# Two common step lists of a two-layer transformer kernel are replaced by others

## The reference

```python
h = _layernorm(x) * (1 + ca) + sa                 # linear attention
qkv = h @ qkv_w + qkv_b                           # q, k, v in 16 heads of 16
q_prime, k_prime = elu(q) + 1.0, elu(k) + 1.0
context = einsum('bhld,bhlde->bhle', q_prime, cumsum(einsum('bhld,bhle->bhlde', k_prime, v)))
norm = einsum('bhld,bhld->bhl', q_prime, cumsum(k_prime))
x = x + ga * ((context / (norm + EPS)) @ out_w + out_b)

h = _layernorm(x) * (1 + cb) + sb                 # coupling network
gf = _global_net(h.mean(axis=1), ...)             # three small layers, one scalar
out = h
for _ in range(3):
    tf = _coupling_net(out, ...)                  # 256 -> 256 -> 128 -> 64 -> 1, gelu between
    coupling = 0.1 + adaptive_range * (0.7 * gf + 0.3 * tf - 0.5) * 2.0
    out = out + coupling * _twist(out)
x = x + gb * out
```

## Time and profile before

| | us |
|---|---|
| median of 3 runs | 1186.86 |
| lowest and highest | 1182.17, 1187.29 |
| profiled execution, its own time | 1183.12 |
| span of the profiled execution | 1181.3 |
| PE busy | 1068.3 (90%) |
| VectorE busy | 735.2 (62%) |
| ScalarE busy | 595.9 (50%) |
| POOL busy | 466.3 (39%) |

### The profile page before, as it was taken

One profiled execution on the slowest core, in us unless ns is written; L12 is line 12 of the kernel. 1 busy time (PEld: TensorE's weight loads), 2 busy tenths in 40 slices (PEclk: granted clock), 3 DMA queues, 4 the chain that ended last, 5 costly groups with the idle time before them and its releaser, 6 DMA issues. The chain is left out here.

```text
span 1181.3 us, 19797 instructions
## 1 busy us (share of the span) xinstructions
PE 1068.3 (90%) x6630; PEld 603.1 (51%) x6630; DVE 735.2 (62%) x1549; ACT 595.9 (50%) x1133; POOL 466.3 (39%) x692
## 2 busy tenths in 40 slices
PE   6699999999999998479999964899999998999996
PEld 3244554454454443346655532556666665455554
DVE  2867878787787783624333322767687873566756
ACT  3157667676767666013333323534444444877742
POOL 2444635444453511068788874433333410000000
PEclk9699999999999999589999996999999999999999
DMA  4521414233250411437676772021211002001001
GB/s 150 98 49 26 87 31 94 65 69 77 55 108 21 74 39 51 151 104 148 154 160 134 152 139 66 1 65 41 77 41 42 19 20 90 1 27 48 34 27 45
DMA packets 73540, 85.05 MB, mean 72 GB/s; under 512 B 12560, under 2 KB 67800, under 8 KB 73312
## 3 DMA queue, kind: packets, MB, share of 16 engines
q1 hardware_dynamic: 61088, 66.99, 21.9%
q0 software_dynamic: 12288, 16.79, 8.4%
q10 hardware_dynamic: 64, 0.02, 0.0%
HBM read 45.31 MB, written 25.21 MB: 60 GB/s over the span
## 5 line engine op out<-in xcount | busy, mean ns | idle before, releaser
L566 DVE TENSOR_REDUCE nmax<-psum 128x1 f32<-128x512 f32 (+3 forms) x352 | 215.5, 636 | 44.5 <-PE psum L790 39.6
L683 ACT ACTIVATE pT<-psum 128x512 f32<-128x512 f32 x320 | 181.1, 596 | 65.7 <-PE psum L811 35.6
L788 PE MATMUL psum<-k6T,q6T 96*128 96x512 bf16 (+3 forms) x512 | 128.3, 311 | 17.8 <-DVE nmax L566 13.5
L808 PE MATMUL psum<-q6T,k6T 99*128 99x512 bf16 x320 | 119.3, 382 | 1.1 <-ACT pT L683 0.9
L1093 POOL DMA_INDIRECT residual<-expert_y,idx_e x64 | 101.0, 1579 | 25.9 <-issue 18.0
L788 PEld LDWEIGHTS psum<-k6T,q6T 96*128 96x128 bf16 x512 | 45.9, 99 | 90.8 <-DVE nmax L566 57.8
L1612 DVE TENSOR_TENSOR l_scores<-psum,const_sb 128x512 f32<-128x512 f32 x128 | 79.5, 683 | 20.3 <-PE psum L1787 20.3
L790 PE MATMUL psum<-negs_bf,ident_bf 128*128 128x128 bf16 (+2 forms) x352 | 88.8, 252 | 0.0
L823 PE MATMUL psum<-pT,v 128*32 128x512 f32 x640 | 85.0, 604 | 0.0
L1080 POOL DMA_INDIRECT expert_tokens<-router_input,idx_e x64 | 63.0, 984 | 49.6 <-POOLq L913 30.4
L1745 PE MATMUL psum<-l_hT,l_w 128*128 128x512 f32 x128 | 63.7, 621 | 0.8 <-ACT l_plus_one L1689 0.8
(11 more groups left out here) (298 smaller groups left out, 2214.0 us busy)
## 6 DMA issues: line engine op xcount, KB each, us to landing
q6T<-q_parts SPq DMA_DIRECT2D x96, 128.0 KB, 4.4
expert_w<-in_ew SPq DMA_DIRECT2D x16, 768.0 KB
x_in<-in_x SPq DMA_DIRECT2D x8, 512.0 KB, 4.3
residual<-x SPq DMA_DIRECT2D x32, 128.0 KB, 1.9
router_input<-h SPq DMA_DIRECT2D x32, 128.0 KB, 1.8
l_x<-residual SPq DMA_DIRECT2D x8, 512.0 KB, 4.9
x_dram<-l_x SPq DMA_DIRECT2D x32, 128.0 KB, 1.7
out<-c_out SPq DMA_DIRECT2D x16, 256.0 KB, 2.1
```

What stands on the lines that cost most here:

```text
L566: dve.tensor_reduce(nmax[:, i, u * nh:(u + 1) * nh], ps_s[:, n % SR, 0:nh * (i + 1) * P].rearrange("p (h k) -> p h k", h=nh), AX_X, ALU.ma ...
L683: act.activation(pT[:, n % PR].rearrange("p h t -> p (h t)"), ps_t[:, n % TR, :], ACT.Exp, scale=HD ** -0.5).then_inc(probs, 1)
L788: pe.matmul(out[:, a, :], q6T[0:6 * HD, b % 2, u * nh + a, i * P:(i + 1) * P], k6T[0:6 * HD, b % 2, 0:w], start=a == 0, stop=False, skip_g ...
L808: last = pe.matmul(out, k6T[:, b % 2, j * P:(j + 1) * P], q6T[:, b % 2, hg * 4:hg * 4 + 4, i * P:(i + 1) * P], start=True, stop=j < i)
```

## The change

Both tables get other numbers. No instruction is added, removed or altered, and the functions that walk the lists stay the same. Since only the order of the sorted list counts, a shift of all numbers means nothing; what changes is the place of the steps relative to each other.

```diff
 LINEAR_PLACE = {
-    "ln": -322, "st": -318, "xn": -303, "hT": [-296, -289],
-    "qk": [-279, -273, -281, -277],
-    "v": [-283, -280, -275, -270],
-    "mask": [-276, -264], "nt": -262, "nb": [-255, -249],
-    "A": [-258, -252, -242, -233],
-    "kt": [-271, -265, -232],
-    "KV": [-251, -238, -225],
-    "PV": [-248, -236, -227, -221],
-    "pr": [-230, -223, -220, -218],
+    "ln": -16, "st": -11, "xn": 11, "hT": [14, 19],
+    "qk": [28, 32, 26, 30],
+    "v": [27, 31, 35, 45],
+    "mask": [36, 39], "nt": 42, "nb": [48, 53],
+    "A": [46, 51, 57, 65],
+    "kt": [34, 38, 43],
+    "KV": [44, 58, 73],
+    "PV": [54, 60, 69, 77],
+    "pr": [59, 76, 85, 88],
 }
 COUPLING_PLACE = {
-    "ln": -143, "st": -136, "xn": -132, "diag": -116,
-    "hT": [[-121, -118], [-112, -104]],
-    "g": {1: -98, 2: -89, 3: -76},
-    "PR": [[[-99, -100], [-114, -110]], [[-92, -96], [-69, -79]]],
-    "L2": [[-86, -83], [-61, -58], [-43, -42]],
-    "L3": [-75, -55, -39], "L4": [-71, -53], "tok": [-63, -45, -37],
-    "up": [[-67, -65], [-49, -46]], "r2": [-59, -60],
-    "fin": -34, "oT": [-33, -32, -30, -29, -26, -24, -9, -6],
+    "ln": -213, "st": -211, "xn": -201, "diag": -166,
+    "hT": [[-196, -189], [-187, -182]],
+    "g": {1: -177, 2: -170, 3: -156},
+    "PR": [[[-178, -181], [-184, -159]], [[-168, -175], [-150, -151]]],
+    "L2": [[-164, -162], [-142, -140], [-123, -121]],
+    "L3": [-158, -137, -119], "L4": [-155, -135], "tok": [-145, -126, -113],
+    "up": [[-149, -147], [-131, -128]], "r2": [-132, -144],
+    "fin": -112, "oT": [-109, -106, -104, -98, -95, -90, -77, -76],
 }
```

More of the change, by code:

```diff
@@ L1281 @@
 LINEAR_PLACE = {
[L1282 to L1285, removed]
-    "qk": [-279, -273, -281, -277],
-    "v": [-283, -280, -275, -270],
-    "mask": [-276, -264],
-    "nt": -262,
-    "nb": [-255, -249],
-    "A": [-258, -252, -242, -233],
-    "kt": [-271, -265, -232],
-    "KV": [-251, -238, -225],
-    "PV": [-248, -236, -227, -221],
-    "pr": [-230, -223, -220, -218],
+    "ln": -16,
+    "st": -11,
+    "xn": 11,
+    "hT": [14, 19],
+    "qk": [28, 32, 26, 30],
+    "v": [27, 31, 35, 45],
+    "mask": [36, 39],
+    "nt": 42,
+    "nb": [48, 53],
+    "A": [46, 51, 57, 65],
[3 more added lines that the diff above has]
+    "pr": [59, 76, 85, 88],
 }
@@ L1845 @@
 COUPLING_PLACE = {
[L1846 to L1849, removed]
-    "hT": [[-121, -118], [-112, -104]],
-    "g": {1: -98, 2: -89, 3: -76},
-    "PR": [[[-99, -100], [-114, -110]], [[-92, -96], [-69, -79]]],
-    "L2": [[-86, -83], [-61, -58], [-43, -42]],
[L1854 to L1860, removed]
+    "ln": -213,
+    "st": -211,
+    "xn": -201,
+    "diag": -166,
+    "hT": [[-196, -189], [-187, -182]],
+    "g": {1: -177, 2: -170, 3: -156},
+    "PR": [[[-178, -181], [-184, -159]], [[-168, -175], [-150, -151]]],
+    "L2": [[-164, -162], [-142, -140], [-123, -121]],
+    "L3": [-158, -137, -119],
+    "L4": [-155, -135],
+    "tok": [-145, -126, -113],
+    "up": [[-149, -147], [-131, -128]],
+    "r2": [-132, -144],
+    "fin": -112,
+    "oT": [-109, -106, -104, -98, -95, -90, -77, -76],
 }
```

## The result

| | before | after |
|---|---|---|
| median of 5 runs, us | 1186.28 | 1177.34 |
| lowest and highest | 1182.17, 1187.29 | 1176.96, 1180.3 |
| ratio, 95% interval | | 0.9947 [0.9929, 0.9965] |
| profiled execution, its own time | 1183.12 | 1177.1 |
| span | 1181.3 | 1175.3 |

The kernel became faster by 0.53%, some 6.3 us by the ratio and 6.0 by the two spans. A later repeat of the new kernel against the one before gave 0.9953 [0.9934, 0.9972]. The forecast was -1.9 us and 1185.0: the right side of zero, a third of the size. The median of 1177.34 lies 0.7 us under the low end of the range, 1178; the ratio, set against the 1186.28 of the kernel before, makes 1180.0, which is inside it. The gain of 0.53% lies at the 0.5% that was to part "within 0.5%" from "faster", and its interval (0.35% to 0.71%) doesn't say on which side.

A forecast was written before the change was run, and what follows sets the result against it. PE was taken as full in both stages' middles, so only gaps could change; -1.1 + 0.2 + 0.3 + 2.0 - 2.1 - 1.2 = -1.9 us gave 1185.0 us, own range 1180 to 1190, whole range 1178 to 1194.

The forecast's parts named there:

- coupling head: Start of the coupling stage: PE stands 6.1 us against 3.4 idle before; taken as +2.0 us.
- last pair: End of the coupling stage: six carried oT steps, waits of 5.4 us with a similar clock loss; -1.2 us.
- (a): Linear stage: A1 starts 3.4 us after A0, last bank free at 3.7; PE loses 0.2 us, seven times: 1.4.
- (b): Linear stage: nt to nb0 needs 3.34 us through VectorE and POOL and has 3.39; loss nothing, or 0.2.
- (c): Linear stage: VectorE ends v1 at 11.5 us, PE wants its bank for v2 at 12.25; no wait, cover 0.7.
- (d): Linear stage: pr1 follows v2 by 1.77 us, the drain of v2 needs 1.57; no wait, 0.2 in hand.
- VectorE late in every cycle: Rival, linear stage: each cycle loses 1.5 us at (a), (c) or (d), 10.5 in seven cycles: 1195.5 us; chance 0.10.
- the rival of late rows for b=4, 6, 7: Rival, linear stage: these loads arrive late too, each costing 4.4 us: +13.3, 1198 us; chance 0.08.
- Late inputs: Linear stage: rows loaded late cost PE 5.1 us for b=3, 1.4 for b=5 and 0.2 for b=7.
- (e): Coupling stage: with a PR step between L2 and L32, L32 takes 1.08 us instead of 1.78; three pairs, -2.1.
- (h): Coupling stage: moving `diag` to before L2, and the last pair's `st` right behind oT7, costs nothing.
- The rival by which the weight loads' share would show room: Rival, both stages: ScalarE's and VectorE's busy times would be the bounds, 72 us: 1115 us; chance 0.02.

## Why the forecast had the side right and the size wrong

The mechanism held, and the sizes of single terms were off: PE stays full in both middles, and only gaps trade places. The new linear cycle is 30.73 us (forecast "near 30.6"), the coupling cycle 42.91 (42.7, and the 0.2 over it has no term), qk2 of sequence 1 starts 33.23 us after the stage's start (33.15), the gap for b=3 is 2.54 us before v1, that before hT00 of the second pair 1.74 (1.9). The terms, against the two profiles:

| term | forecast | measured | how |
|---|---|---|---|
| linear head | -1.1 | -1.0 | 33.23 for 33.15 |
| linear middle | +0.2 | -1.6 | six cycles from qk2 of sequence 1 take 190.2 us for 6 x 30.45 = 182.7, 7.5 and not 9.1; in the old list 191.85, 9.1 and not 8.9 |
| linear end | +0.3 | +0.7 | 20.7 for 20.3 |
| coupling head, clock aside | +2.0 | +0.5 | waits of 4.3 and not 6.1 |
| clock at that head | 0, at most +1.5 | +3.0 | 30.16 us against 27.18 at full clock, and full clock in the first profile before |
| L32 | -2.1 | -2.1 | 1.08 us for 1.78, three times |
| last pair | -1.2 | -3.7 | below |
| stages ahead | 0 | -1.7 | not the change's |

The measured terms make -5.9, the spans differ by 6.0. What no term holds is -0.2 us in the linear stage and +0.1 in the coupling stage. All these are one execution against one. The second trace of the kernel before has 2.9 us of low clock at its coupling head too, so most of the +3.0, like the -1.7, is an accident of the two executions; that the two partly cancel and leave the spans' 6.0 close to the ratio's 6.3 is luck.

**Linear middle.** (a) was right in kind and a little small, 0.27 us a cycle for 0.2, of which 0.18 show in A1 itself; A1 closer behind A0 shows that this is the mask products' distance. (b), (c) and (d) came out at nothing, as said; the rival "VectorE late in every cycle" and the rival of late rows for b=4, 6, 7 did not happen, but the run with A1 half a microsecond closer (3.9 us slower) shows how near the first one was. Late inputs cost 4.3 us in the cycle with b=3 where I had 5.1: the wait of 2.54 and the low clock behind it are there, the second loss of 0.5 before v2 is not (in the second trace of the new kernel it is there, 0.50). For b=5 I had 1.4; the cycle loses 1.25 in all, and 0.58 of that stays when the rows come early, so 0.7. For b=7 nothing shows. The extra work on VectorE came out as counted, 0.9 for 1.0. The miss of this term is therefore in the late rows, 1.7 us too much, less 0.3 too little in (a). What the new list gains here is that extra work: the old list's three cycles with it are 4.7 us over, and the wait of 0.70 before `nt` belongs to them as well as the three before pr; the new one's are 1.6 over, both with the late rows of b=5 in them.

**Coupling head.** The 0.5 behind the table load and the 0.3 before L3 did not appear, and the wait before L2 was 0.16, not 0.9. This step erred to the slow side by 1.5 us.

**L32.** (e) was right to the tenth, though the old L32 did not stand right behind L2: `g2` is between them, the likely reason for its 1.78 where nothing between makes it 1.92.

**Last pair.** This is the step that failed most: "waits 0.1, 0.9, 2.5, 1.15 and 0.8: 5.4, with a similar clock loss". Measured are 0.79, 0.42, 1.04 and 0.78, 3.0 in all, behind a clock loss of 1.4 us in the oT products, so 4.4 without it. The old list had 6.5 us of waits and 1.7 in the eight L2 products. That is 4.4 against 8.1: -3.7. So of the 2.5 us by which the term was too small some 1.7 are the "similar clock loss", which costs nothing in the new list, and the rest are waits, 4.4 and not 5.4 at full clock. The 2.5 us before the second update's L2 is 1.85 at full clock (in the run with the coupling table alone). And the clock loss falls into the oT products ahead of that wait, which absorbs it. More traces bear this out: from the last pair's fourth transpose step to the start of the last oT group, all five with the new coupling table unaltered take 61.5 us, two of them at full clock in those oT products and three at low clock; five with the old order of the last pair take 65.6 to 66.7. The work in that stretch is the same to some 0.1 us by start-to-start times. The size and place of the single waits are read from traces; a separate experiment on the last pair alone did not succeed, since carried oT steps bring the load's wait with them.

**The clock at the coupling head** hid most of this in the profiles. By times, which average over executions, the coupling table is worth 5.6 us, and its terms without the head's clock make 0.5 - 2.1 - 3.7 + 0.1 = -5.2. Two traces in 14 have full clock there, those of the kernel before first taken and of the version with later loads, and the latter has it low one step later; both tables have it low in others. It costs the old table 1.4 to 2.9 us there in six traces and the new one 2.7 to 3.0 in five, so some 0.8 of the 5.2 go to it, and 4.4 are left, within the interval by time. The forecast left that 0.8 out; the other 2 us are in the comparison of one profile with one.

**(h).** No wait of PE shows behind `diag` and `st` in the new table. The runs with carried oT steps suggest that this hangs on their being moved together: with xn in its old place PE loses a wait of 6 us, with xn moved and `diag` not, more.

**The rule on busy time.** The rival by which the weight loads' share would show room gave 1115 us; the middle cycles have 20.49 us of weight loads in 30.73 and no wait, and no order tried here brought one under 30.4. The headroom that the Trainium skill (Perfetto Trace Analysis, Identifying the Most-Contended Engine) reads from the weight loads' share was not to be had by another order in this stage; whether other products would use it, no run here shows.

## What to carry to other kernels

Where the busiest engine is full in the steady state, a new order is worth what it does at the first and the last round, where a partner has extra work (3.7 of the microseconds by which the new linear list leads the old one with the late rows gone, against 1.6 that it loses in its undisturbed cycles), and where a step's inputs come just before it: give the last round something to do in its waits, and put one other step between a producer and a consumer that needs two results at once. Steps that hang together through the queues (store, load, statistics, normalisation, gates) are best moved together: the table that moves them all gained 5.6 us, carrying the oT steps alone lost 10, and carrying them with xn but without `diag` lost 21. Look first at what the load queue issues ahead of the rows that are waited for: moving ten loads here gave as much as the whole new order, and added to it.

## What the runs showed of the hardware that I had not expected

The granted clock falls in different executions of one program in different places. At the head of the coupling stage, behind the same gaps (1.25, 0.96 and 0.96 us), the 512-column products of the kernel before took 1.98 us for a group of four in one execution and 3.78 in another; the second is the lower of the two levels (1.2 for 2.4 GHz) for one group and part of the next. One profile against one can so be off by 3 us of 1180 either way.

A low clock in front of a wait cost nothing here: 16 oT products took 3.46 us instead of 2.03, and the wait behind them 0.42 instead of 1.85. The same two rows at full clock, from the kernel with the coupling table alone:

```profile
1154.42 2.03 PE L2298 MATMUL psum<-c_gate_diag,c_x0T 128*128 128x128 f32 x16
1158.30 1.96 PE L2266 MATMUL psum<-c_a,c_w 128*128 128x512 f32 x4 [1.85 <-ACT c_a L2217]
```
